# Local attention layers: ScalarE's order of a gate copy, the attention rows' copy, the squares and the gelus

## The reference, cut to what matters

```
h = shift_token(x);  q, k, v = split(h @ wqkv)          # 8 heads of 64
q = l2norm(q) * qs;  k = l2norm(k) * ksc;  q, k = rotary_xpos(q, k)
o = local_attention(q, k, v)                             # windows of 64, each looks one back
x = x + o @ wo
h = layernorm(shift_token(x)) * lg + lb
a, g = split(h @ w1 + b1)                                # 2 x 341 columns
x = x + (a * gelu(g)) @ w2 + b2
```

## Time and profile before

| | us |
|---|---|
| median of 3 runs | 1847.09 |
| lowest, highest | 1846.87, 1849.22 |
| the profiled execution | 1842.65 |
| its span, first to last instruction | 1840.8 |
| granted TensorE clock, mean | 0.981 |

### The profile page before, as it was taken

One profiled execution on the slowest core, in us unless ns is written; L12 is line 12 of the kernel. 1 busy time (PEld: TensorE's weight loads), 2 busy tenths in 40 slices (PEclk: granted clock), 3 DMA queues, 4 the chain that ended last, 5 costly groups with the idle time before them and its releaser, 6 DMA issues. The chain is left out here.

```text
span 1840.8 us, 54091 instructions
## 1 busy us (share of the span) xinstructions
PE 1729.1 (94%) x22916; PEld 1097.3 (60%) x22916; DVE 1443.2 (78%) x2658; ACT 1408.2 (76%) x1737; POOL 1430.2 (78%) x851
## 2 busy tenths in 40 slices
PE   5999999999999999999999999986899999978997
PEld 2466666666666666666666666675566666653454
DVE  5888888888888888888888887525988888855785
ACT  2688888888888888888888889943898888853463
POOL 6699999999999999999999999974765566634122
PEclk9899999999999999999999999998999999999998
DMA  5101010101010110101010100041121111110000
GB/s 143 25 20 31 19 31 22 28 24 30 22 29 24 26 30 20 30 24 28 23 31 19 28 19 11 2 149 28 42 45 37 37 37 37 33 26 0 1 0 24
DMA packets 71080, 56.89 MB, mean 31 GB/s; under 512 B 29196, under 2 KB 64184, under 8 KB 70840
## 3 DMA queue, kind: packets, MB, share of 16 engines
q1 hardware_dynamic: 70840, 53.44, 11.5%
HBM read 14.54 MB, written 1.05 MB: 8 GB/s over the span
## 5 line engine op out<-in xcount | busy, mean ns | idle before, releaser
L278 POOL TENSOR_TENSOR ah_probs_lo<-ah_probs,ah_probs_hi 128x1024 f16<-128x1024 f32 x512 | 1072.6, 2133 | 79.4 <-ACT ah_probs L487 79.2
L542 DVE TENSOR_REDUCE ah_part_max<-ah_p_m 128x1 f32<-128x512 f32 x1024 | 668.6, 685 | 121.7 <-PE ah_p_m L342 111.4
L484 ACT ACTIVATE ah_probs_hi<-ah_p_s 128x1024 f16<-128x1024 f32 x512 | 531.2, 1038 | 190.1 <-PE ah_p_s L358 178.9
L487 ACT ACTIVATE ah_probs<-ah_p_s 128x1024 f32<-128x1024 f32 x512 | 532.5, 1040 | 0.0
L372 PE MATMUL ah_p_o<-ah_v_hi,ah_probs_hi 128*128 128x65 f16 x4096 | 470.3, 194 | 5.7 <-POOL ah_probs_lo L278 5.1
L374 PE MATMUL ah_p_o<-ah_v_lo,ah_probs_hi 128*128 128x64 f16 x4096 | 470.3, 193 | 0.0
L376 PE MATMUL ah_p_o<-ah_v_hi,ah_probs_lo 128*128 128x65 f16 x4096 | 470.1, 194 | 0.0
L372 PEld LDWEIGHTS ah_p_o<-ah_v_hi,ah_probs_hi 128*128 128x128 f16 x4096 | 382.8, 98 | 84.2 <-DVE a_attn L565 12.3
L374 PEld LDWEIGHTS ah_p_o<-ah_v_lo,ah_probs_hi 128*128 128x128 f16 x4096 | 378.3, 98 | 91.4
L342 PE MATMUL ah_p_m<-ah_k_hi_lo,ah_q_hi_twice 128*128 128x512 f16 x1024 | 393.6, 385 | 7.1 <-DVE ah_part_max L542 3.7
L357 PE MATMUL ah_p_s<-ah_q_hi_twice,ah_k_hi_lo 128*128 128x512 f16 x1024 | 388.7, 380 | 0.8 <-ACT ah_probs L487 0.4
(11 more groups left out here) (318 smaller groups left out, 3074.9 us busy)
## 6 DMA issues: line engine op xcount, KB each, us to landing
ba_v_skew<-ba_v_own SPq DMA_DIRECT2D x64, 129.0 KB, 2.3
ah_q_hi_twice<-ah_hi SPq DMA_DIRECT2D x128, 64.0 KB, 2.0
ah_k_hi_lo<-ah_hi SPq DMA_DIRECT2D x64, 64.0 KB, 1.9
ah_one_k_hi<-ah_hi SPq DMA_DIRECT2D x64, 64.0 KB, 2.0
ah_k_hi_lo<-ah_lo SPq DMA_DIRECT2D x64, 64.0 KB, 2.0
ah_max_q_lo<-ah_lo SPq DMA_DIRECT2D x64, 64.0 KB, 2.0
ah_w_head<-in_w_heads SPq DMA_DIRECT2D x16, 160.0 KB, 2.4
bw_rot<-in_rot SPq DMA_DIRECT2D x4, 512.0 KB, 8.1
```

Of the source, the lines that this page charges most:

```text
L278: pool.tensor_tensor(pl[:, p % RW, :, :], pb[:, p % RP, :, :], ph[:, p % RW, :, :], ALU.subtract).then_inc(lo_pool, 1)
L484: act.activation(ph[:, p % RW, :, :], p_s[:, p % 2, :, :], ACT.Exp, scale=HD ** -0.5)
L487: act.activation(pb[:, p % RP, :, :], p_s[:, p % 2, :, :], ACT.Exp, scale=HD ** -0.5).then_inc(exp_done, 1)
L542: dve.tensor_reduce(part[:, t, 2 * half + b:2 * half + b + 1], p_m[:, b, :], AX, ALU.max).then_inc(maxed, 1)
```

## The change

In the steps r = 0 of groups 0 to 5 ACT gets another order; nothing is added or taken away. The copy of gate 1 goes ahead of the copy of the attention rows (it stood behind the Sqrt). The two gelus go behind the two squares of the next tile, that is into the next step (they stood at the end of this one). The copy of gate 2 stays where it was, behind the Sqrt.

```diff
--- before.py
+++ after.py
@@ -1315,6 +1315,12 @@
                         act.activation(g_sb[0:n, k, :], gate_bank(m, k)[0:n, :], ACT.Gelu,
                                        bias=lw.b1[0:n, l, 1, k:k + 1]).then_inc(g_copied, 1)
 
+                def gelu_early(m):
+                    act.wait_ge(g_copied, HC * (m + 1))
+                    act.activation(g_sb[:, 0:HC - 1, :], g_sb[:, 0:HC - 1, :], ACT.Gelu)
+                    act.activation(g_sb[0:LASTN, HC - 1, :], g_sb[0:LASTN, HC - 1, :],
+                                   ACT.Gelu).then_inc(gelu_done, 1)
+
                 for j in range(-2, STEPS_B):
                     u = j
                     if on(u):
@@ -1323,6 +1329,9 @@
                             if u >= 1:
                                 act.wait_ge(ssq_done, u)
                             act.activation(sq[:, s, :], p_qk[:, s, :], ACT.Square).then_inc(squared, 1)
+                    m, r = geglu_of(j - 1)
+                    if r == 0 and m < LATE_G:
+                        gelu_early(m)
                     u = j - 2
                     if on(u):
                         act.wait_ge(st_ready, u + 1)
@@ -1370,6 +1379,7 @@
                         if u >= 2:
                             act.wait_ge(v_ready, u - 1)
                         act.activation(hTh[:, u % 2, :], p_e[:, 0:P], ACT.Copy).then_inc(hTh_done, 1)
+                    copy_gate(j, 1)
                     u = j - 3
                     if on(u):
                         act.wait_ge(at_turned, u + 1)
@@ -1382,16 +1392,10 @@
                         if j >= 1:
                             act.wait_ge(rooted, j)
                         act.activation(std[:, :], ssqc[:, :], ACT.Sqrt).then_inc(std_done, 1)
-                    copy_gate(j, 1)
                     copy_gate(j, 2)
                     m, r = geglu_of(j)
                     if r == 0 and m >= LATE_G:
                         gelu_late(m)
-                    elif r == 0:
-                        act.wait_ge(g_copied, HC * (m + 1))
-                        act.activation(g_sb[:, 0:HC - 1, :], g_sb[:, 0:HC - 1, :], ACT.Gelu)
-                        act.activation(g_sb[0:LASTN, HC - 1, :], g_sb[0:LASTN, HC - 1, :],
-                                       ACT.Gelu).then_inc(gelu_done, 1)
 
             @block.vector
             def _(dve):
```

## The result

The changed kernel takes 1855.68 us (median of 7 runs, 1849.72 to 1858.9), the kernel before 1846.87 us on the same chip (7 runs, 1843.06 to 1851.79). The ratio is 1.0043, with a 95% interval of 1.0024 to 1.0062. The forecast was 1848.3 us, with a range up to 1852.4: it was wrong.

The account below looks back on a forecast made before the run. ACT up to the v copy, then DVE from its remainder of v, bounds steps r = 0 and 1. Five groups at +0.29 us and the first at -0.26 give +1.2 us on 1847.09: 1848.3 us, range 1844.2 to 1852.4.

Parts of the forecast that it names:

- What bounds the steps: Steps r = 0 and 1, 26.0 us: ACT up to exps and v copy, then DVE from its remainder of v.
- Part 1: Gate 1's copy ahead of atT, steps r = 0: second group's atT 1.24 us late, gate 2 +0.17 us.
- Part 2: Gelus behind the next tile's squares: exps 0.24 us later after gate 2's copy; DVE's rotation 2.8 us sooner, costed at nothing.
- The sum of the schedule: Shift of DVE's remainder of v: +0.29 us for five groups, -0.26 for the first, giving +1.2 us.
- The steps behind move with it unchanged: After the remainder of v, later steps shift equally, because DVE is full from there and releases PE and ACT.
- DVE's early work: DVE's rotation starts 2.8 us sooner but is costed at nothing, since its remainder of v must wait for ACT's v copy.
- the terms that no row fixes: Unknown costs in the groups: ACT's new wait up to 8.2 us in all; below, -3.0 us if squares never waited.
- Rival B: At PE's `out_project`, late atT isn't absorbed: everything behind late by 1.36 us a group, 8 us, 1855 us; chance 10%.
- Rival A: Steps r = 0 and 1: DVE's gap is worth its length, 16 us over six groups, 1831 us; chance 6%.

Follow-up runs that it names:

- the filled kernel: Twenty unused PE matmuls added in each of the six r = 1 gaps, against the changed kernel; 1845.59 us, ratio 0.9999 to before; again 1846.57 us, 0.9991.
- part 1 alone: Only gate 1's copy moved ahead of the attention rows' copy, against the kernel before; 1844.56 us, ratio 0.9984; again 1843.81 us, 0.9986.
- part 2 alone: Only the gelus moved behind the squares, gate 1's copy at its old place, against the kernel before; 1851.15 us, ratio 1.003.
- half filled: Ten unused PE matmuls added in each of the six r = 1 gaps, against the changed kernel; 1847.88 us, ratio 1.0012 to before.

## Why the prediction was wrong

- **What bounds the steps: right.** ACT up to the v copy, then DVE from its remainder of v. DVE's gap became 1.28 us (forecast 1.3), the new one 2.82 (2.8), steps r = 0 in the second group are 2.78 shorter (2.7), steps r = 1 at full clock 2.98 longer (3.0).
- **Part 1: right in mechanism, the loss a little too large.** atT came 1.26 later (1.24), gate 2's copy 0.07 (0.17): PE needed 1.75 us from atT to gate 2, not 1.84.
- **Part 2: right.** 6.09 us from the copy of gate 2 to the exps, as worked out.
- **The sum of the schedule**: +1.2 us forecast for six groups, of which groups 0 to 4 have +0.9; +0.28 measured for these five with the gap filled. The remainder of v came 0.15 us later where +0.29 was forecast.
- **The step that failed** is the one after it: "The steps behind move with it unchanged". I costed DVE's early work at nothing because the remainder of v bounds it, and looked at what the early work gains on DVE, not at what it does on PE. The forecast has no term for TensorE's clock; against the kernel with the gap filled, that term measured 6.75 us in the local layers (3.26 + 3.49, below). PE's own waits were in the trace, and those that move (1.11, 0.88 and some 0.5 in small pieces) could have been added up to the gap of 2.5. What it does to the clock no row of before showed, so its size couldn't be forecast; but PE is busy at a granted clock of 1.00 in those steps, and a fallen clock belonged among the terms that no row fixes.
- **The size of that term**: of the 8.65 us that the local layers lost from step 10 on, the schedule of groups 0 to 4 is 0.28, the falls in groups 0, 2 and 4 are 1.11 + 1.09 + 1.06 = 3.26 (each against the filled kernel), and from the first squares of the last group to the end the changed kernel is 3.49 over the filled one, 2.25 of it ahead of the last down projection and 1.24 in it. The other 1.62 the filled kernel has there as well, 1.31 of it in the down projection, which took 4.25 us for 2.94. That part is not explained.
- **Rival B gave 1855 us, and that is the measured time, for a wrong reason.** Its marks were a copy of gate 2 over 0.5 us later and exps over 6.5 us behind it; neither came (0.07 and 6.09), and part 1 alone costs nothing. A time that fits doesn't show its mechanism.
- **Rival A** fell as expected: DVE's gap of 4.28 us was cut by 3.0 and the step pair not shortened (26.21 us in the second group, before 26.01).

The filled kernel shows that PE's idle time in that gap is the cause of most of the loss: the only thing added is unused work on PE. It doesn't show that the length of the single wait is what counts, and not how busy PE is over the step. The Trainium skill says of TensorE's clock ("TensorE: Matmul & The Clock Gate", section Part 1: The HAM clock gate) that throttled is the default state and activity releases it; by that rule the traces agree, at 0.89 with the gap and 1.00 with it filled.

**Left open**: which gap brings a fall. The changed kernel had it in groups 0, 2, 4 and 5 in both traces, part 2 alone in all but group 2, half filled in 1 and 3, part 1 alone in group 4 in one trace and in 0 and 3 in the other, with no such gap. The one trace of before had no fall in these steps, but that execution lies 4.2 us under its median, so others may have had some. Also open is why the last down projection is slow: it took 2.94 us in the three traces with the gelus at their old place, and 4.10 to 5.49 in the nine with the gelus moved. What PE did just ahead doesn't explain it: over the 14 us before it, PE was busy for 9.25 us in the kernel before and for 9.24 in the filled one, both at a clock of 1.00. Open, too, is where part 1's 0.16% lies. Filling PE's waits in part 1's order wasn't tried.

## What to carry to other kernels

When work is moved earlier on one engine, follow it to the matrix engine as well: add up which of its waits run together, and give a longer single wait a price: here 1.1 us for most falls of the clock in the changed kernel (0.5 to 2.4 in part 1's order), with falls at 15 of 21 such waits in four traces, though the sum of its waits in the step grew only from 2.50 to 3.05 us. Moving idle time from one engine's gap to another's gains nothing while two paths of nearly equal length meet at the next step. To test whether a gap matters by the clock, fill it with unused matmuls and change nothing else, and look first in the page's count of instructions that they ran: a condition that is never true looks like a filling without effect.

## What the runs showed of the hardware

- In the changed kernel TensorE's clock fell in four of six places although PE's work had only been moved. In the second group, where the clock held, PE was busy over steps r = 0 and 1 for 22.25 us of 26.21 (11.07 + 11.18), before for 22.79 of 26.01 (14.04 + 8.75). The waits had become one of 2.5 us in place of several of up to 1.1. With work of no use in that gap (2.21 us of it) the clock stayed at 1.00 in 15 of 15 places, without it it fell in 15 of 21. With waits of 1.1 us at most it still fell in 3 of 18.
- With all else equal, unused work made a kernel 0.43% faster (1.0042 to 0.9999).
- Behind one and the same wait of 3.1 us, 24 matmuls took 2.94 us in three traces and 4.10 to 5.49 in nine; one and the same program had 4.25 and 4.50.
